# S4 plus mixture-of-experts layer on eight cores: four chunks of the experts' first matmuls moved from the output projection into the convolution-kernel stage, and a second set of table buffers

## What is computed

```python
# S4 branch: a long convolution per channel, by FFT
kern = 2.0 * einsum('hn,hnl->hl', coef, exp(dtA[:, :, None] * arange(L))).real
y = irfft(rfft(xn) * rfft(kern))[:, :L]
y = gelu(y + xn * D)
a, g = split(y @ W_out + b_out, 2)
s4 = a * sigmoid(g)
# expert branch: 16 experts (all computed, weighted by a top-2 gate) and a shared one
h = silu(xn @ We1 + be1) * (xn @ We3 + be3)
moe = sum_e combine[e] * (h_e @ We2_e + be2_e) + shared(xn)
```

## Time and profile before

| | us |
|---|---|
| runs timed (2) | 9690.88 and 9740.01, median 9715.44 |
| the profiled execution, own time | 9770.83 |
| its span on core 5, the slowest | 9769.3 |
| spans of the other seven cores | 9607.1 to 9742.2 |
| busy in the span: TensorE / VectorE / ScalarE / GpSimd | 4859.9 / 4186.7 / 2331.1 / 1790.1 |
| mean granted TensorE clock, cores 0 to 3 / 4 to 7 (medians) | 0.708 / 0.696 |

### The profile page before, as it was taken

The page is one execution under the profiler, slowest core; times in us unless marked ns, Lnnn a source line. Parts: engine busy times, 40 slices in busy tenths (PEclk is TensorE's granted clock), DMA queues, the critical chain, the costliest instruction groups (busy, mean ns, idle before and its releaser), DMA issues.

```text
span 9769.3 us, 88125 instructions; the slowest of 8 cores (9607.1 to 9769.3 us)
## 1 busy us (share of the span) xinstructions
PE 4859.9 (50%) x26752; PEld 2701.1 (28%) x26752; DVE 4186.7 (43%) x6602; ACT 2331.1 (24%) x3354; POOL 1790.1 (18%) x3087
## 2 busy tenths in 40 slices
PE   0100079665656756746633333332665555566652
PEld 0100034332322323323311111111222245455552
DVE  7155520245453454354255555554223134444443
ACT  1011023333333333434333333332222100000000
POOL 1000022233333333333322222221111100000000
PEclk9955578776766767767755555555677777778876
DMA  3601223222222212212211111111110365554568
GB/s 135 141 17 29 34 70 82 54 60 50 55 49 55 61 36 59 60 44 63 61 27 27 27 27 28 26 28 43 50 39 35 73 122 97 103 109 108 108 111 204
DMA packets 753014, 637.18 MB, mean 65 GB/s; under 512 B 241089, under 2 KB 653121, under 8 KB 751506
## 3 DMA queue, kind: packets, MB, share of 16 engines
q0 software_dynamic: 173088, 345.61, 14.0%
q1 hardware_dynamic: 475490, 259.72, 12.3%
q10 hardware_dynamic: 103968, 26.22, 1.6%
HBM read 398.38 MB, written 267.52 MB: 68 GB/s over the span
## 4 chain that ended last, share of the span: by engine, by line
PE 35%; DVE 26%; DMA 16%; ACT 9%; issue 7%; POOL 3%; SPq 1%; DVEq 1%; ACTq 1%; another core or an unknown queue 1%; POOLq 0%
PE PS L1469 10%; PE PS L1474 10%; PE PS L1659 9%; DMA p_h<-dH 6%; POOL dKLOC L1020 3%; DMA dH<-p_h 2%; PE PS L1360 2%; DMA p_w<-we 2%; ACT L1175 2%; DMA dKLOC<-p_xbuf 2%; PE PS L1129 1%; DMA p_x<-x 1%; DVEq L188 1%; DVE p_h L1677 1%; ACT p_gbuf L1175 1%
## 5 line engine op out<-in xcount | busy, mean ns | idle before, releaser
L1469 PE MATMUL PS<-xnF,p_w 128*128 128x512 bf16 x4608 | 1257.7, 423 | 975.8 <-ACT p_h L1497 917.3
L1659 PE MATMUL PS<-p_h,p_w 128*128 128x256 bf16 x8192 | 992.1, 289 | 669.8 <-DVE p_h L1683 550.7
L1474 PE MATMUL PS<-xnF,p_w 128*128 128x512 bf16 x4608 | 1224.3, 414 | 0.0
L1659 PEld LDWEIGHTS PS<-p_h,p_w 128*128 128x128 bf16 x8192 | 844.3, 103 | 817.6 <-issue 679.4
L1469 PEld LDWEIGHTS PS<-xnF,p_w 128*128 128x128 bf16 x4608 | 486.9, 106 | 1645.0 <-issue 1427.0
L1002 DVE TENSOR_TENSOR p_tw<-p_gbuf,s_t1r 128x512 bf16<-128x512 bf16 x128 | 54.4, 425 | 1953.9 <-ACT p_gbuf L978 1953.8
L1677 DVE SCALAR_TENSOR_TENSOR p_h<-p_h,sb_be_t,p_s 128x256 bf16<-128x256 bf16 x1024 | 495.8, 484 | 796.7 <-DMA p_h<-dH 701.8
L1020 POOL DMA_DIRECT2D dKLOC<-p_xbuf x1024 | 599.7, 766 | 1095.2 <-ACT p_xbuf L987 1077.6
L1155 PE MATMUL PS<-s_i1a,p_ybuf 128*128 128x256 bf16 x512 | 208.5, 407 | 1010.0 <-DVE p_ybuf L1227 1010.0
L1474 PEld LDWEIGHTS PS<-xnF,p_w 128*128 128x128 bf16 x4608 | 483.3, 105 | 651.1 <-issue 419.7
L1493 ACT ACTIVATE p_s<-PS,sb_be_t 128x512 bf16<-128x512 f32 x512 | 351.8, 687 | 1296.5 <-DMA dH<-p_h 737.0
(11 more groups left out here) (255 smaller groups left out, 7841.0 us busy)
## 6 DMA issues: line engine op xcount, KB each, us to landing
dS<-p_s POOLq DMA_DIRECT2D x576, 128.0 KB, 2.1
dH<-p_h POOLq DMA_DIRECT2D x576, 128.0 KB, 2.3
p_s<-dS SPq DMA_DIRECT2D x256, 256.0 KB, 3.3
p_h<-dH SPq DMA_DIRECT2D x256, 256.0 KB, 4.4
p_w<-we POOLq DMA_DIRECT2D x48, 1024.0 KB, 12.2
p_x<-x SPq DMA_DIRECT2D x64, 512.0 KB, 6.0
dKLOC<-p_xbuf POOLq DMA_DIRECT2D x1024, 32.0 KB, 2.0
p_k<-dKLOC POOLq DMA_DIRECT2D x512, 64.0 KB, 2.3
```

The lines of the kernel that those rows point to most:

```text
L1469: ins = t.matmul(b1, w1b[u % 2][:, dc * 512 + ic * 128: dc * 512 + ic * 128 + 128], cx.xnF[:, dc * L + ts * 512: dc * L + ts * 512 + 512], ...
L1474: ins = t.matmul(b3, w3b[u % 2][:, dc * 512 + ic * 128: dc * 512 + ic * 128 + 128], cx.xnF[:, dc * L + ts * 512: dc * L + ts * 512 + 512], ...
L1659: ins = t.matmul(og, wsrc[:, ic * H + dc * 128: ic * H + dc * 128 + 128], buf[:, ic * 256:ic * 256 + 256], start=False, stop=(e == 16 and ...
```

## The change

Two edits. First, `BM` becomes two sets that groups use in turn, and SyncE's loads of group `g_` now wait for the 18 instructions of group `g_ - 2`. Second, the loop of stage 2 places 24 chunks instead of 20, by `(g_ * 24) // 32`, and stage 4 places none; `p5_close` moves to the end of stage 2, and the chunk's optional first wait on TensorE (`qsnap`) goes.

```diff
@@ emit_p2
-        BM = {nm: S2_("p2c_" + nm, [64, 256], BF16) for nm in
-              ["pr", "pi", "wr", "wi", "qr", "qi", "ar", "ai"]}
+        BM = [{nm: S2_(f"p2c{j}_" + nm, [64, 256], BF16) for nm in
+               ["pr", "pi", "wr", "wi", "qr", "qi", "ar", "ai"]} for j in range(2)]
...
                 if g_ >= 1:
-                    sync.wait_ge(cv.h, cv0 + (g_ - 1) * DVg + 18)
                     sync.wait_ge(swk.h, swk.val)
+                if g_ >= 2:
+                    sync.wait_ge(cv.h, cv0 + (g_ - 2) * DVg + 18)
                 for pl, nm in enumerate(FPL):
                     src = ap(dF8, pl * 8192 + g_ * 256, [(65536, 64), (1, 256)])
-                    sync.dma_start(out=BM[nm][:], in_=src).then_inc(swk.h, 16)
+                    sync.dma_start(out=BM[g_ % 2][nm][:], in_=src).then_inc(swk.h, 16)
...
-            for c5 in range(8 + (g_ * 20) // 32, 8 + ((g_ + 1) * 20) // 32):
+            for c5 in range(8 + (g_ * 24) // 32, 8 + ((g_ + 1) * 24) // 32):
                 p5_chunk(cx, st5, c5)
-    cx.st5 = st5
+    p5_close(cx, st5)
...
@@ emit_p4
-            if tb % 2 == 1:
-                p5_chunk(cx, cx.st5, 28 + tb // 2, qsnap=snap if tb == 1 else None)
-    p5_close(cx, cx.st5)
     cx.p4_done = True
...
@@ p5_chunk
     @block.tensor
     def _(t):
-        if qsnap is not None:
-            quiesce(cx, t, qsnap)
         for n in range(lo, hi):
```

More of the change, by code:

```diff
@@ L874, in _ @@
                     v.wait_ge(ct.h, pe0g - DPEg + 4)
-                bview = lambda t_: ap(BM[t_], 0, [(256, 64), (8, 32), (0, 8), (1, 8)])
-                aview = lambda t_: ap(BM[t_], 0, [(256, 64), (8, 32), (1, 8), (0, 8)])
+                bview = lambda t_: ap(BM[g_ % 2][t_], 0, [(256, 64), (8, 32), (0, 8), (1, 8)])
+                aview = lambda t_: ap(BM[g_ % 2][t_], 0, [(256, 64), (8, 32), (1, 8), (0, 8)])
                 sview = lambda t_: ap(t_, g_ * 32, [(H, 64), (1, 32), (0, 8), (0, 8)])
@@ L1440, in p5_setup, with p5_chunk @@
     return st
-def p5_chunk(cx, st, ci, qsnap=None):
+def p5_chunk(cx, st, ci):
     block, PS = cx.block, cx.PS
```

## The result

| | us | forecast |
|---|---|---|
| before, median of 16 runs | 9696.28 (9629.48 to 9752.66) | |
| changed, median of 17 runs | 9616.38 (9491.12 to 9693.11) | 9622, range 9545 to 9705 |
| ratio | 0.9892, 95% interval 0.9852 to 0.9933 | 0.990 |

What follows compares the result with a forecast made beforehand. No engine was taken to bound the kernel; who waits in each period counts, with chunks partly exposed in stage 2 and almost wholly in stage 4. -267 + 174 + 0 = -93 us, from 9715.4 to 9622, range 9545 to 9705.

Steps and rivals of the forecast that it cites:

- The sum: Whole kernel: -267 + 174 = -93 us, to 9622 us from the median; ends -163 and -35.
- Chunks leave stage 4: Stage 4: from 890.5 us to eight plain blocks of 77.9, 623.5 us; 267 us go, ends 255 and 283.
- Chunks come into stage 2: Stage 2's 30 periods: 22 instead of 18 hold a chunk; four grow by 43.5 us each, 174 us come.
- My low end of 130: Stage 2's added chunks: at the fastest chunk periods, such as 100.05 us, four cost 32.6 each, 130 us in all.
- Two sets of tables: Stage 2's table loads: only VectorE's 9.9 us idle before the first table product could shrink; taken as 0.
- What I said wouldn't change: Plain period stays at 67.4 us, chunk periods within 5 us; stages 3, 6 and 7, untouched, within 30 us.
- the plain period: Stage 2, a group with no chunk ahead of it: 67.4 us from one first table product to the next.
- the 30 that I allowed: Stages 3, 6 or 7, untouched by the change: a move of over 30 us would show the prediction wrong.
- Rival 1: Stage 2 gets denser, more chunk time at 0.81 clock: +220 instead of +174, net -47, 9668 us; chance 0.13.
- Rival 2: Stage 4's bursts fall from 35.1 to 30.9 us, stage 2's added chunks cost 32.6 each: net -171, 9544; chance 0.08.
- Rival 3: Stage 4 goes cold: bursts of 54.6 us at 1.2 GHz against 35.1, +156, net +63, 9778 us; chance 0.04.
- Rival 4: Chunks were hidden in stage 4 after all; the change only adds 174 us in stage 2: 9889 us; chance 0.02.

Runs made afterwards that it cites:

- the second chip: The changed kernel, unaltered, run once more on another chip as the study's final run: 9787.3 us, ratio 1.012 to that chip's before.
- the mixed kernel: Kernel before, with stage 4's four chunks kept there but each cut into eight pieces between the tanh instructions: 9686.5 us, beside a before of 9845.1.
- the two-table kernel: Kernel before with only the two sets of tables and the shifted wait of their loads, chunks unmoved: 9818.1 us, ratio 1.013.

## Why the prediction came out

**The total** was forecast at -93 us (-1.0%) and came out at -80 between the medians (-1.1% by the ratio), -130 between the two profiled executions. It is right, but part of that is luck: the second chip gave +1.2%, outside my range, because the executions compared there had different clocks. The sum had no term for that.

**Chunks leave stage 4: -267 forecast, -280 measured**, within the ends of 255 and 283. The cause is the one I read from the earlier trace rows, ScalarE's order; the mixed kernel shows it, since the same chunks cost 120 us less there without leaving the stage. The 13 us over the forecast go with shorter bursts: they take 30 to 33 us (mean 31.4) now, where those of the five plain blocks that I averaged took 34.4 in the mean.

**Chunks come into stage 2: +174 forecast, +122 measured** on the core that ended last, +135 at the full clock, +192 at the low one. This is the term that was mis-sized. I took 43.5 us per chunk as the mean of 18 periods, "with every stall on stores and weight loads in it". That mean was right for the core and the execution from which it came. What it mixes are three prices: 98.4 - 67.4 = 31 us for a bare chunk at the full clock, 11 more when a weight load falls into it with tiles still to come, and 7 to 14 more at 0.81. The first and the second carry over to another run; the third belongs to the run, and a mean taken on the slowest core takes it at its worst. My low end of 130 assumed only fast chunks and counted no weight loads; core 6 lies under it because its extra chunks came with more of the full clock (0.75 against 0.69 over the stretch).

**Two sets of tables: 0 forecast, 0 to 1 measured.**

**What I said wouldn't change:** the plain period kept its 67.4 us and stage 3 its time. The rest of stage 2, behind the last group, gets 8 to 11 us shorter, which I had not counted: by the code its two chunks are the last ones now, and no weights are left to load in them. Stages 6 and 7 moved by 49 us, over the 30 that I allowed. Between the cores of one execution they range from 2004 to 2099 us before and from 2043 to 2127 after (means 2065 and 2095), and the two-table kernel, which has before's chunks, has a mean of 2117, so this doesn't count against the sum; the bound was set without looking at the other cores.

**The rivals.** Rival 1 (more chunk time at 0.81, +220, 9668) is not what the first chip did, and its size is nearly what core 0 of the second showed: +192. The price of 0.81 is real and bigger than the change. But that a denser stage 2 brings it is not shown: cores 2, 3, 6 and 7 of that same execution ran the same 22 chunks without any time at 0.81, and so did six of the eight cores of the profiled kernel with 32 chunks in the loop. By the shifts above, what counts is also what the other pair of the die is doing, stages 6 and 7 included, which neither the rival nor the sum had. The Trainium skill's limit in "TensorE: Matmul & The Clock Gate" (section "Seeing it yourself"; three cores of a die with dense matmuls bring the whole die to 13/16) agrees with the level of 0.81 and with the die as its unit, once the pairs' records are shifted (623 us against 7); that it takes three cores, no run here shows. Core 0's 0.70 and core 2's 0.78 over the same stretch of the program in the last run don't speak against it, since they ran it 4782 us apart. Rival 2's bursts came true in part (30 to 33 us). Its cheap chunks came only where no weight load falls into them; over the 22 chunk periods the mean was 103.7 us at the full clock, 36 each. Rival 3 (cold bursts, 54.6) is refuted by 31.6 us behind 79 us of idleness. Rival 4 (hidden chunks) is refuted by stage 4's 280 us.

## What to carry to other kernels

Work that fills an engine's gap costs its own length less what the other engines do beside it, so the place of a chunk decides its price: here 61 to 68 us alone, 60 to 70 behind another engine's order, 31 to 54 beside VectorE's tables, some 15 to 20 in halves beside the table steps, and 3 in small pieces beside the power steps, which leave TensorE idle. In each place look at what stands behind the inserted work on *all* its engines (evictions ahead of a tanh, stores ahead of a store), and cut it into pieces no longer than the gap. A change of 1% is read by stage, between cores with the same granted clock, and never from one total.

## What the hardware showed

- The same program spent 2822 us in 30 periods at a mean granted clock of 0.78 and 3020 at 0.70. The level differs between executions, chips and cores of one execution, and made this stretch 199 us longer. In the profiled execution of the kernel with a chunk in every period all eight cores had 0.775 to 0.779 over the whole span; in two other executions of it they had 0.725 to 0.756.
- A die's clock comes down to 0.81 and goes back up for all four cores at once, while its two pairs of cores run the same program 428 to 5797 us apart in the profiled executions of before and after. So a core's stage 2 can be slowed while the other pair is in stages 6 and 7.
- A section that begins with a branch brought a table load of 1.28 us on ScalarE even where the table is unchanged: 64 loads ahead of the tanhs in the mixed kernel, 8 in the changed one.
- The loads of an expert's weights, 1 MB tiles that take 12 us to land (median), delay the chunk's stores of 128 KB, from 2.3 to 13.4 us, enough to cost a chunk with two staging tiles some 11 us, and one with four about 5.
- The plain period of stage 2 took 67.3 to 68.3 us in every trace. TensorE's granted clock over it was 0.50 to 0.55 on all cores, so these runs don't show what another clock would do to it.
